# A scan stage rewritten for chunks of 128 tokens and groups of 16 images, on one Trainium2 core

## What is computed

```python
# recurrent layer (Wx is batch-normalised over all tokens)
def step(yt, wx_t):
    yt = sigmoid(wx_t + yt @ V.T)
    return yt, yt
_, ys = scan(step, y0, swapaxes(Wx, 0, 1))       # 3136 steps, batch 64

# gated filter on x = layernorm(residual); c = 64 complex channels
forget_gate = sigmoid(x @ Wf + bf + 2.0)
input_gate  = sigmoid(x @ Wi + bi)
delta       = softplus(x @ Wd + bd) * 0.1
A, B        = fft2 of padded 7 x 7 kernels, A scaled by 0.95 * sigmoid(|A|) / |A|
Bx          = B * x                              # complex product, per pixel and channel
inp         = delta * input_gate * Bx            # real and imaginary part apart
# then T = 16 steps of h <- forget * (A h) + inp, written in closed form by repeated squaring
```

## Time and profile before

| | |
|---|---|
| time, median of 3 runs | 16452.49 us (16402.66 to 16489.39) |
| the profiled execution | 16475.65 us, its span 16473.9 us |
| PE busy | 11190.3 us, 68% of the span |
| DVE busy | 12515.2 us, 76% |
| ACT busy | 10361.8 us, 63% |
| POOL busy | 4296.3 us, 26% |
| scan stage, its place in the span | from about 5209 to 13581 us |

### The profile page before, as it was taken

How to read it: one execution, slowest core, us unless ns; L and a number is a source line. 1 busy time by engine, 2 the same in 40 slices (tenths; PEclk the granted TensorE clock), 3 DMA queues, 4 the chain that set the end, 5 groups by cost and what they waited for, 6 DMA issues and landing times. The chain is left out here.

```text
span 16473.9 us, 269631 instructions
## 1 busy us (share of the span) xinstructions
PE 11190.3 (68%) x86216; PEld 8358.9 (51%) x86216; DVE 12515.2 (76%) x28025; ACT 10361.8 (63%) x24318; POOL 4296.3 (26%) x4365
## 2 busy tenths in 40 slices
PE   7888888888887555555555555555555537777888
PEld 5666666666665333333333333333333315555788
DVE  6777777777774799999989899899989995554133
ACT  7888888888885555555555555555555547776200
POOL 4444444444443111111111111111111112211000
PEclk9999999999997666666666666666666666766555
DMA  3333333333332111111111111111111113333399
GB/s 73 80 80 84 86 86 80 80 80 81 86 85 63 34 39 40 38 38 41 38 38 40 38 38 40 38 38 38 41 38 38 33 28 95 95 93 85 103 314 313
DMA packets 2117075, 1191.51 MB, mean 72 GB/s; under 512 B 50565, under 2 KB 2098376, under 8 KB 2107604
## 3 DMA queue, kind: packets, MB, share of 16 engines
q1 hardware_dynamic: 1702548, 967.89, 23.4%
q10 hardware_dynamic: 409600, 205.55, 4.3%
q0 software_dynamic: 3648, 2.20, 0.0%
HBM read 708.85 MB, written 466.62 MB: 71 GB/s over the span
## 5 line engine op out<-in xcount | busy, mean ns | idle before, releaser
L1186 PEld LDWEIGHTS s_pW<-s_U,s_vh 128*128 128x128 f32 x6272 | 1445.6, 260 | 2499.3 <-ACT s_U L1077 2118.8
L1186 PE MATMUL s_pW<-s_U,s_vh 128*128 128x64 f32 x6272 | 1453.3, 325 | 1427.4 <-ACT s_U L1077 1424.8
L1077 ACT ACTIVATE s_U<-s_pW,s_zb 128x64 f32<-128x64 f32 x3136 | 981.5, 313 | 2126.3 <-PE s_pW L1186 2065.1
L1228 PE MATMUL s_pG<-s_wg,s_XNT 128*112 128x384 f32 x3584 | 1879.2, 614 | 5.2 <-ACT s_Z L1130 5.2
L831 POOL TENSOR_TENSOR s_rst<-s_var,s_epst 112x8 f32<-112x8 f32 x224 | 231.0, 1031 | 6063.5 <-DVE s_var L80 6063.5
L1095 ACT ACTIVATE s_XN<-s_X,s_nmr,s_rst 112x128 f32<-112x128 f32 x1792 | 735.0, 481 | 882.5 <-POOL s_nmr L835 882.5
L409 ACT ACTIVATE KB<-pV,qkb 32x392 f32<-32x392 f32 x2048 | 1189.8, 581 | 25.7 <-PE pV L499 1.9
L1221 PE MATMUL s_pN<-s_ident,s_XN 112*128 112x112 f32 x896 | 219.7, 401 | 1247.4 <-ACT s_XN L1095 1247.4
L1171 PE MATMUL s_pY<-s_ident,s_U 128*112 128x128 f32 x1792 | 414.1, 370 | 936.9 <-DVE s_X L950 936.7
L249 POOL TENSOR_TENSOR SS<-SS,mx 128x784 f32<-128x784 f32 x512 | 769.5, 1503 | 801.9 <-DVE mx L342 801.9
L1164 PE MATMUL s_pW<-s_XT,s_ws 128*128 128x448 f32 x896 | 789.1, 973 | 30.3 <-issue 29.6
(11 more groups left out here) (246 smaller groups left out, 34208.8 us busy)
## 6 DMA issues: line engine op xcount, KB each, us to landing
XL<-in_x_dram SPq DMA_DIRECT2D x64, 1568.0 KB, 12.4
XR<-in_x_dram SPq DMA_DIRECT2D x64, 1568.0 KB, 18.1
x_dram<-XR SPq DMA_DIRECT2D x64, 1568.0 KB, 8.1
xh_dram<-XH SPq DMA_DIRECT2D x64, 1568.0 KB, 8.1
s_X<-x_dram SPq DMA_DIRECT2D x224, 448.0 KB, 5.3
s_XQ<-xh_dram ACTq DMA_DIRECT2D x448, 224.0 KB, 2.7
x_dram<-s_IN SPq DMA_DIRECT2D x224, 448.0 KB, 4.0
r_X<-x_dram SPq DMA_DIRECT2D x64, 1568.0 KB, 14.2
```

What stands on the lines that cost most here:

```text
L1077: act.activation(U[j.par][:, t, :], pW[t // R % 2][:, B * (t % R):B * (t % R) + B], ACT.Tanh, bias=zb[:, 0:1], scale=0.5).then_inc(u_sb, 1)
L1186: pe.matmul(pW[t // R % 2][:, B * (t % R):B * (t % R) + B], vh[:], before, start=False, stop=True, skip_group_check=True).then_inc(z_ps, 1)
L1228: pe.matmul(pG[i % 3][0:T, 0:3 * C], XNT[:, i, :], wg[:], start=True, stop=True).then_inc(g_ps, 1)
```

## The change

All of it is in `scan_phase`.

- A chunk is TF = 128 tokens; there are NCH = 25, of which the last has 64. A group is OS = 16 images: NO = 4 groups a chunk, 100 in all, on 128 partitions by 16 x 128 values. A chunk has 4 slots of K = 32 steps. An input matmul serves R = 8 steps (512 columns).
- `XU`, two buffers of [C, TF, B], takes the place of `XT` and `U`: the turned inputs of a chunk are written into it, and each state overwrites the inputs of its token.
- TG has one buffer, XN lies in the buffer of `f1`, the loads of x1 have three buffers (NX) and not four.
- Work per group is cut into four quarters of 4 images (Q, NQ) where it was two halves.
- No loop and no `Image` objects: all slots are written out by the generator `slots`.
- The places of the other work move to the new k; the power for the magnitude stands behind the group's three operations on POOL, and its tanh on ACT at k = 25 of the third slot. DVE takes the four residual additions between the first four operations of the arithmetic, and the product with the forget gate before the second complex product.

```diff
+    TF = 128
+    OS = 16
+    NCH = (S + TF - 1) // TF
     NO = B // OS
-    SLOTS = 8
-    NX = 4
-    K = T // SLOTS
-    R = K // 2
+    NX = 3
+    K = TF // NO
+    R = 8
-    Q = OS // 2
+    Q = 4
+    NQ = OS // Q
-        XT = [sb(f"XT{i}", [C, B, T]) for i in range(2)]
-        U = [sb(f"U{i}", [C, T, B]) for i in range(2)]
+        XU = [sb(f"XU{i}", [C, TF, B]) for i in range(2)]
-        TG = [sb(f"TG{i}", [T, 4, OS, HC]) for i in range(2)]
+        TG = sb("TG", [TF, 4, OS, HC])
+        XN = pairs["f1"][:].rearrange("t r b c -> t (r b c)").rearrange("t (b c) -> t b c", b=OS)
+        def slots():
+            for j in range(-1, NCH + 2):
+                for s in range(NO):
+                    g = (j - 1) * NO + s
+                    if g <= NGR:
+                        yield (j, s, g if 0 <= g < NGR else None, g - 1 if 1 <= g else None,
+                               0 <= j < NCH, j + 1 < NCH)
+        def steps_at(j, s, k):
+            n = size(j) // NO
+            return [n * s + i for i in range(n) if i * K // n == k]
```

DVE, ahead of the statistics:

```diff
+                    did(dve.tensor_tensor(t0, tf[:, 0], tf[:, 1], ALU.add))
+                if conv:
+                    residual(oc, tc, 0)
+                if o is not None:
+                    did(dve.scalar_tensor_tensor(d0, tf[:, 1], 1.0, a2, ALU.add, ALU.mult))
+                if conv:
+                    residual(oc, tc, 1)
...
+                if conv:
+                    residual(oc, tc, 3)
+                    statistics(oc, tc)
...
+                    dve.wait_ge(am, o * NA + 5)
+                    did(dve.scalar_tensor_tensor(t2, d1, 2.0, t2, ALU.mult, ALU.subtract))
+                    if conv:
+                        dve.wait_ge(n_ps, oc * NQ + NQ)
+                    did(dve.scalar_tensor_tensor(f1[:, 1], t1, -1.0, d1, ALU.add, ALU.mult))
```

ACT:

```diff
+            def keep_turned(j, s, q):
+                n = j + 1
+                i = (n * NO + s) * NQ + q
+                b0 = OS * s + Q * q
+                act.wait_ge(xt_ps, i + 1)
+                if j >= 1:
+                    act.wait_ge(y_ps, i - 2 * NO * NQ + 1)
+                act.copy(XU[n % 2][:, 0:size(n), b0:b0 + Q].rearrange("c t b -> c b t"),
+                         pX[:, 0:Q * size(n)].rearrange("c (b t) -> c b t", b=Q)).then_inc(xt_sb, 1)
+                load_xq(i + 2)
+            def gate(oc, tc, i):
+                act.wait_ge(g_ps, oc * OS + i + 1)
+                if i == 0:
+                    wait(act, dv, (oc - 1) * NV + 9)
...
+                    if prep and k in (1, 4, 7, 10):
+                        keep_turned(j, s, k // 3)
+                    if conv and 10 <= k < 10 + NQ:
...
+                    if o is not None and k == 20:
+                        if conv:
+                            act.wait_ge(bx_d, oc + 1)
+                        act.activation(f1[:, 0], t1, ACT.Square, bias=cols[0:tm, 2:3]).then_inc(am, 1)
+                    if o is not None and k == 22:
+                        needs(11)
+                        act.wait_ge(am, o * NA + 6)
+                        act.activation(t1, t2, ACT.Square, bias=cols[0:tm, 2:3]).then_inc(am, 1)
+                    if conv and k > K - OS:
+                        gate(oc, tc, k - (K - OS) - 1)
```

PE:

```diff
-                pe.matmul(pW[r % 2][:, 0:R * B], ws[:], XT[j.par][:, :, R * r:R * r + R].rearrange("c b t -> c t b"),
+                pe.matmul(pW[r % 2][:, 0:R * B], ws[:], XU[j % 2][:, R * r:R * r + R, :].rearrange("c t b -> c (t b)"),
...
+                    if conv and k in (1, 3, 5):
+                        turn_u(oc, (k + 1) // 2)
+                    if conv and s + 1 < NO and k == K - 2:
+                        turn_u(oc + 1, 0)
+                    if prep and k in (0, 3, 6, 9):
+                        turn_inputs(j, s, k // 3, oc)
+                    if conv and 11 <= k < 11 + NQ:
...
+                        turn_normal(oc, tc, k - 11)
+                    if conv and k >= K - OS:
+                        i = k - (K - OS)
```

More of the change, by code:

```diff
@@ L722, in scan_phase, with tokens @@
         ee = XNT[:].rearrange("p a b -> p (a b)")[:, 6 * C:7 * C]
[L723 to L746, removed]
+        fld = [XU[0][:].rearrange("p a b -> p (a b)")[:, i * C:i * C + C] for i in range(6)]
+        def slots():
[8 more added lines that the diff above has]
+            return [n * s + i for i in range(n) if i * K // n == k]
+        def tokens(dram, b0, n, j):
+            return dram[b0:b0 + n, j * TF:j * TF + size(j), :].rearrange("b t c -> t b c")
         @block.sync
@@ new lines, in turned_by, with residual, statistics @@
+                dve.tensor_tensor(flat(out[0:tc]), flat(out[0:tc]), flat(Dl[0:tc]), ALU.add).then_inc(sem_, 1)
+            def residual(oc, tc, q):
+                dve.wait_ge(y_ps, oc * NQ + q + 1)
+                v = X2[oc % NX][0:tc, Q * q:Q * q + Q, :]
+                dve.scalar_tensor_tensor(v, pY[0:tc, :].rearrange("t (b c) -> t b c", b=Q), 0.5, v,
+                                         ALU.mult, ALU.add).then_inc(x2_d, 1)
+            def statistics(oc, tc):
+                dve.wait_ge(x2_d, oc * NQ + NQ)
+                wait(dve, ag_d, oc)
+                for i in range(OS):
+                    w = dve.bn_stats(st[0:tc, i, :], X2[oc % NX][0:tc, i, :])
+                w.then_inc(st_d, 1)
+                dve.wait_ge(st_d, oc + 1)
+                wait(dve, rs_d, oc)
+                moments(dve, st[0:tc], mean[0:tc], var[0:tc], tmp[0:tc], mo_d, oc * 2, ag_d, -0.5)
@@ L1044, in _ @@
+                if scan and s == NO - 2:
+                    bounded(j)
         @block.scalar
@@ new lines, in turn_normal @@
+            def turn_normal(oc, tc, q):
+                pe.wait_ge(xn_d, oc * NQ + q + 1)
+                wait(pe, n_sb, oc * NQ + q - 1)
+                for i in range(Q):
+                    w = pe.transpose(turned_bank[q % 2][:, tc * i:tc * i + tc], XN[0:tc, Q * q + i, :], ident[0:tc, 0:tc])
+                w.then_inc(n_ps, 1)
+            for j, s, oc, o, scan, prep in slots():
+                conv = oc is not None
+                tc = size(oc // NO) if conv else 0
+                if scan and s == 0:
+                    inputs(j, 0)
+                for k in range(K):
+                    if scan:
+                        for t in steps_at(j, s, k):
+                            wait(pe, u_sb, j * TF + t)
+                            before = XU[j % 2][:, t - 1, :] if t else XU[1 - j % 2][:, TF - 1, :]
```

673 lines of the change are left out of this document (313 added, 360 removed).

## The result

The changed kernel takes 14879.75 us (median of 4 runs, 14843.06 to 14929.4) where the kernel before takes 16427.89 beside it: a ratio of 0.9061, 95% interval 0.9043 to 0.9078. The profiled execution took 14929.4 us, its span is 14927.6 us. The forecast was 15,020 with a range from 14,600 to 15,850.

A forecast was written before the change was run, and what follows sets the result against it. DVE was taken as the bound: 99 slots of W = 66.9 us, less 26, are 6597 for 8096.5; with start, tail and landing net -1435 from 16475.65, so 15,040, and 23 lower for the median: 15,020 us, range 14,600 to 15,850.

The forecast's parts named there:

- The bound and DVE's work: Scan stage: DVE is the bound, its work a slot going from 33.64 us to 62.8 us.
- the 29 us: Straight code: DVE's "issue" waits, 10 of 2.6 us, go; 0.12 us a slot, which the sum keeps as work.
- Waits at the head: Slot's first DVE operations: PE, at the low clock, turns states late; waits of 1.6 us (quarter 2) and 1.5 (quarter 3).
- W: Time of a new slot in the scan stage: 62.8 + 1.6 + 1.5 + 1.0 = 66.9 us.
- The last square: ACT's square `t1` after k = 22: done at 45.5, DVE asks at 44.5, a wait of 1.0 us.
- The ring: PE, ACT and POOL beside DVE: XN starts at 21, is done by 29.5, BX due at 31.8; no wait.
- 16 lie at 3.7 by the line through these: POOL's power for 16 elements: 3.7 us, from 2.50 for 8 and 10.93 for 64; 1.2 us more.
- The gates: From k = 16, about 33.3 us into the slot: first 4 us at the low clock, sixteen gates end near 57.
- low clock: Rival: PE stays at 0.50 through all gates, W = 73.4, +640 us, 15,660; chance 0.18.
- no overlap: Rival: at k = 16 to 31 steps and gates cease to overlap, W = 82.7, about 16,580; chance 0.06.
- The strided copy: ACT's copy of turned inputs, 512 elements: between 0.62 and 1.04 us, W unchanged; rival three times as dear, 15,180, 0.05.
- Start, tail, landing: First chunk and its following slot +37 us, last group's arithmetic to the store +25, landing of a larger store 3 more.

The follow-up runs named there:

- experiment 1: Changed kernel with chunks of 112 tokens for 128 (112 groups for 100): 15774.78 us, 0.957 of the kernel before.
- experiment 5: Changed kernel with all 18 DVE operations of 2048 elements written as two of 1024: 14932.23 us, 0.9075 of the kernel before.
- experiment 6: Changed kernel with a spare power of 16 elements on POOL ahead of the group's own: 15325.54 us, 0.9316 of the kernel before.
- experiment 3: Changed kernel with each of ACT's four strided copies of turned inputs done twice: 14937.11 us, 0.9069 of the kernel before.
- experiment 7: Changed kernel with input matmul at step 6, turnings at k = 1, 2 and 3, last square at k = 21: 14628.77 us, 0.8896 of the kernel before.
- experiment 10: Changed kernel with 9 spare PE matmuls after the last gate and 9 at k = 1: 14713.96 us, 0.8939 of the kernel before.

## Why the prediction was right, and where not

*The bound and DVE's work.* Right to 0.3%: 62.60 us a slot for 62.8. The line through 512 and 1024 elements held at 2048, 128 partitions were free (experiment 1), and the half chunk cost as much as a full one. One reading was wrong and harmless: the 0.12 us a slot of "issue" stand among the 2.67 us of waits, so the work of 33.64 had already left them out, and no term of the sum holds the 29 us that it was said to keep. The straight code has no such wait; that it was the loop's branch is argued from its count.

*Waits at the head.* 2.02 us for 3.1. The first was about right (1.49 in the slot shown, 1.4 in the mean, for 1.6). The second was mis-sized: 0.76 in the slot shown and 0.6 in the mean, for 1.5. The step that failed took PE to be at the low clock until quarter 3. It had the high clock's length 6.3 us after the first turning (0.77 for 1.16), so the quarter was there at 8.9 us and not at 9.75. The trace of before had a sign of it that was not read: in the slot of the earlier trace rows a step's record takes 0.43 us at 9024.98, 5.1 us after the turning, where the low clock's is 0.69, and in the next slot the turning of inputs takes 0.56 at 9058.34 for 0.95 at 9023.04. In the slot after that PE is still at the low clock at 9095.59 (0.69), 5.1 us after its turning, so before the change it went either way. The two waits together are 1.1 of the 1.4 us that W is short of 66.9.

*The last square.* 0.82 for 1.0, and at the place forecast: due at 43.3, done at 44.2, for 44.5 and 45.5. The work gave 0.2 more, and the 0.10 at L991 was not in the sum.

*The ring.* No wait on XN came, as forecast, but that was luck: XN was done at 30.5 for 29.5 and due at 30.8 for 31.8, 0.3 us of room for 2.3. Statistics began 0.7 us early, and POOL's chain took 9.0 us for 5.7. The failed step is "16 lie at 3.7 by the line through these", and that the other two operations stay as they were. The prices read from the trace of before were those beside DVE operations of 1.2 us, and there the line is right (3.78 in experiment 5); DVE's operations doubled, and that holds all three of POOL's up. What was read as POOL's price was in good part DVE's: with DVE idle, at the start of the stage, the power takes 1.65 us for 8 elements and 10.57 for 64 in the kernel before, and 2.92 for 16 in the changed one. Beside DVE's work it took 2.62 for 8 and 4.94 for 16 in the slots read. Past that room each us costs 99: experiment 6 waited 4.2 us a slot and took 420 us more.

*The gates.* First gate at 33.6 for 33.3, last one taken off at 54 for 57, 0.87 us a step and, from 38 us into the slot to the last gate, a clock of 1.00: both rivals at this place (low clock, no overlap) are out. The first 4.4 us of gates were at the low clock, for the 4 assumed. The first tanh fell 4.5 us before t0 for 3.

*The strided copy.* I took the lower end, 0.62; it is 1.03, the upper end. The time didn't move, as the cover was real (experiment 3). The same change of layout made the input matmul shorter, 0.59 us a record at its best for 0.91, which at the high clock was not in the sum either.

*Start, tail, landing.* 5491.7 for 5453.59 is +38 (+37 forecast); the tail +21 (+25). In sum 15,040 less 14,929 are 111 us: 6597 forecast for the slots against 6488 is 109 of them.

## What to carry to other kernels

When one engine is busy nine tenths and the others wait for it, price its instructions one by one at the new size: that sum was right to 0.3% and decided the case. What that sum leaves open are the waits where the other engines' programs meet it; they are cheap to move once their place is known (by the ratios, the few numbers changed in experiment 7 gave 270 us more, and the spare matmuls of experiment 10 gave 200). And when operations of one engine get longer, look at the engine beside it: a chain of tiny POOL operations that takes 3.4 us with DVE idle took 9.0 beside it, and with that the room that the plan had counted on.

## What the runs showed of the hardware that I had not expected

- POOL's operations on 128 x 16 elements took 2.20, 4.95 and 1.88 us beside DVE operations of 2.29 us, 1.13, 3.78 and 0.88 beside ones of 1.2 (both with two inputs from SBUF), and 0.22, 2.92 and 0.22 with DVE idle.
- Two independent halves of a DVE operation of 2048 elements follow each other at 2.36 us for 2.29: 0.07 us, where the line through 512 and 1024 elements has 0.148 for one operation more.
- ACT writing 512 elements 256 bytes apart took 1.03 us, 2.0 ns an element; 448 contiguous ones took 0.52, 1.2 ns each. The Trainium skill, page "SBUF — State Buffer", section "Door 1: The DMA port swizzle", says that each access to a new line of 16 bytes pays. The write agrees, at 0.8 ns an element more.
- A matmul record that reads 512 contiguous columns took 592 ns at its shortest, one of 448 columns 448 bytes apart 910: 1.16 ns a column for 2.03. At the low clock the two cost alike, 1.97 and 2.02 ns (2.02 us over two records for 1.81).
